# Attention and three graph layers on one core: source scores added by VectorE, own-branch products formed in the layer that uses them

## What is computed

```python
# attention
el, er = scores of every node (8 heads x 4 kinds); em = e_pro @ attn_m
e = (sum_t (el[src] + er[dst] + em) * mask) / 3.0;  e = where(e > 0, e, 0.2 * e)
a = exp(e - max over dst) / sum over dst
rst = segment_sum(feat_src[src] * a, dst)
# each of the three layers
msg = relu(h @ pW + pb)[src]
mean = segment_sum(msg, dst) / max(deg, 1)
out = mean @ lW + lb + h @ rW        # the own branch is h @ rW + lb
h = silu(out / norm(out))            # last layer: layernorm instead of silu
```

## Time and profile before

| | us |
|---|---|
| median of 3 runs | 3454.67 (3454.27 to 3454.99) |
| the profiled execution, its own time | 3451.81 |
| its span, first to last instruction | 3450.0 |
| first gather of the attention (POOL) | 101.68 |
| first gather of the layers | 1457.72 |

### The profile page before, as it was taken

The page is one execution under the profiler, slowest core; times in us unless marked ns, Lnnn a source line. Parts: engine busy times, 40 slices in busy tenths (PEclk is TensorE's granted clock), DMA queues, the critical chain, the costliest instruction groups (busy, mean ns, idle before and its releaser), DMA issues. The chain is left out here.

```text
span 3450.0 us, 44783 instructions
## 1 busy us (share of the span) xinstructions
PE 2900.8 (84%) x12845; PEld 1770.6 (51%) x12845; DVE 1542.9 (45%) x5381; ACT 1377.4 (40%) x3235; POOL 2527.9 (73%) x2655
## 2 busy tenths in 40 slices
PE   7688877777777777199999997999999888999984
PEld 5577656656555655044455553444555433445542
DVE  6399655555555556113333232232333423445445
ACT  5366655555554555033333332333333322222220
POOL 2677777777777777777777776777777767777775
PEclk9688988888888888599999999999999999999995
DMA  7898766666666664166666654666666456667663
GB/s 218 228 281 256 204 171 178 171 169 174 179 168 177 173 169 125 42 195 182 184 194 194 201 173 143 183 180 183 199 196 201 147 171 190 197 199 221 208 187 108
DMA packets 491898, 631.26 MB, mean 183 GB/s; under 512 B 163477, under 2 KB 402096, under 8 KB 491648
## 3 DMA queue, kind: packets, MB, share of 16 engines
q0 software_dynamic: 122192, 324.68, 34.0%
q1 hardware_dynamic: 340848, 277.92, 27.2%
q10 hardware_dynamic: 28608, 25.71, 2.3%
HBM read 558.00 MB, written 70.05 MB: 182 GB/s over the span
## 5 line engine op out<-in xcount | busy, mean ns | idle before, releaser
L1218 POOL DMA_INDIRECT ring<-message_table,src_index x1545 | 1469.8, 951 | 502.5 <-issue 481.1
L1269 PE MATMUL ps<-ring,attention_work 128*128 128x384 f32 (+1 forms) x2940 | 1149.5, 538 | 85.3 <-DMA attention_work<-message_table 75.1
L604 POOL DMA_INDIRECT ring<-attention_table,src_index x784 | 763.1, 973 | 245.6 <-issue 245.2
L1269 PEld LDWEIGHTS ps<-ring,attention_work 128*128 128x128 f32 x2940 | 551.5, 192 | 555.7 <-issue 286.4
L1814 PE MATMUL ps<-ring,one_hot 128*128 128x265 f32 x1568 | 533.1, 458 | 19.7 <-issue 18.6
L1580 ACT ACTIVATE ring<-one_hot 128x384 f32<-128x384 uint8 (+1 forms) x735 | 362.0, 553 | 195.7 <-PE ps L1269 132.9
L1814 PEld LDWEIGHTS ps<-ring,one_hot 128*128 128x128 f32 x1568 | 314.7, 221 | 85.6 <-issue 49.6
L1339 PE MATMUL ps<-ring,attention_work 128*32 128x256 f32 x3090 | 256.6, 402 | 103.7 <-DMA ring<-message_table,src_index 103.4
L613 POOL DMA_INDIRECT dense_adjacency<-times,cell x277 | 269.5, 973 | 84.4 <-issue 84.4
L1434 DVE SCALAR_TENSOR_TENSOR block_o<-ps,inv_deg,root 128x256 f32<-128x256 f32 x147 | 71.1, 484 | 546.8 <-PE ps L1307 546.8
L1783 PE MATMUL ps<-ring,ident 128*128 128x224 f32 x224 | 95.7, 519 | 254.7 <-DMA ring<-attention_table,src_index 254.6
(11 more groups left out here) (185 smaller groups left out, 3500.7 us busy)
## 6 DMA issues: line engine op xcount, KB each, us to landing
attention_work<-message_table SPq DMA_DIRECT2D x360, 256.0 KB
attention_work<-in_dst_edges SPq DMA_DIRECT2D x112, 448.0 KB
ring<-message_table,src_index POOLq DMA_INDIRECT x1545
one_hot<-dense_adjacency SPq DMA_DIRECT2D x63, 336.0 KB, 4.0
one_hot<-dense_adjacency SPq DMA_DIRECT2D x42, 448.0 KB, 4.5
attention_sums<-sums_out SPq DMA_DIRECT2D x112, 132.5 KB
dense_adjacency<-root SPq DMA_DIRECT2D x14, 952.0 KB
ring<-attention_table,src_index POOLq DMA_INDIRECT x784
```

What stands on the lines that cost most here:

```text
L604: pool.indirect_dma_start(m.ring[:, k, t, 0:cols], None, table, bass.IndirectOffsetOnAxis(ap=m.src[:, at:at + 1], axis=0)).then_inc(s[f"ro ...
L1218: pool.indirect_dma_start(m.quad_ring[:, k, j, :], None, m.tables[w.l], bass.IndirectOffsetOnAxis(ap=m.src[:, t:t + 1], axis=0)).then_inc( ...
L1269: last = nc.tensor.matmul(m.ps[:, 2 + half, 0:cols], m.m_rows[:, u % HELD_ROWS, half * P:(half + 1) * P], m.a_rows[:, k, 0:cols], start=(j ...
```

## The change

Three edits.

1. **Source scores.** `left_of` and its identity product are gone from PE. DVE adds the source scores from the gathered rows to the bank and writes the sum to SBUF (`kinds`); the mask multiply then has both inputs in SBUF. Chunk c+3's feature product on PE now waits for that addition of chunk c+2, no longer for the mask multiply.
2. **Own branch.** ACT copies the turned h straight into `root`, which now keeps h transposed. `project` forms 256 columns, the message alone, and DVE adds one bias there. `combine` forms the own branch in the other half of its bank first, ahead of the wait for `merged`; DVE adds its bias in a new instruction after `lmm` and then does the scaled addition. The wait for the zero stores goes from DVE to ACT.
3. **Transposes.** The third transpose of `to_heads` takes 64 edges.

```diff
@@ layers, tensor: combine and project
+            pe.wait_ge(s["o"].sem, s["o"].free(w.slot0 + i))
+            for k in range(2):
+                nc.tensor.matmul(m.ps[:, 0, D:2 * D], m.root[:, n, k * P:(k + 1) * P], m.w_pr[:, w.l, k, D:2 * D],
+                                 start=(k == 0), stop=(k == 1))
             pe.wait_ge(s["merged"].sem, s["merged"].done(w.chunk0 + (q - 1 if q is not None else WORK - 1)))
-            pe.wait_ge(s["o"].sem, s["o"].free(w.slot0 + i))
...
-                last = nc.tensor.matmul(m.ps[:, 5, :], m.b_hT[:, k * P:(k + 1) * P], m.w_pr[:, w.l + 1, k, :],
+                last = nc.tensor.matmul(m.ps[:, 5, 0:D], m.root[:, w.block(i), k * P:(k + 1) * P], m.w_pr[:, w.l + 1, k, 0:D],
@@ layers, vector: first and second
-                nc.vector.tensor_tensor(m.l_msg[:, u % 2, :], m.ps[:, 5, 0:D], m.bias[:, w.l + 1, 0:D], ALU.add)
-                nc.vector.tensor_tensor(m.root[:, n, :], m.ps[:, 5, D:2 * D], m.bias[:, w.l + 1, D:2 * D],
+                nc.vector.tensor_tensor(m.l_msg[:, u % 2, :], m.ps[:, 5, 0:D], m.bias[:, w.l + 1, 0:D],
                                         ALU.add).then_inc(s["evac"].sem, 1)
...
-            nc.vector.scalar_tensor_tensor(m.b_o[:], m.ps[:, 0, 0:D], m.inv_deg[:, n:n + 1], m.root[:, n, :],
+            nc.vector.tensor_tensor(m.b_o[:], m.ps[:, 0, D:2 * D], m.bias[:, w.l, D:2 * D], ALU.add).then_inc(s["rooted"].sem, 1)
+            dve.wait_ge(s["rooted"].sem, s["rooted"].done(u))
+            nc.vector.scalar_tensor_tensor(m.b_o[:], m.ps[:, 0, 0:D], m.inv_deg[:, n:n + 1], m.b_o[:],
@@ attention, tensor
-                pe.wait_ge(s["masked"].sem, s["masked"].done(c - 1))
+                pe.wait_ge(s["added"].sem, s["added"].done(c - 1))
...
-        def left_of(c):
-
-            rows_in(pe, c)
-            nc.tensor.matmul(m.ps[:, 0, 0:TILES * 32].rearrange("p (t n) -> p t n", t=TILES), m.ident[:],
-                             m.ring[:, c % RING, :, WIDE:ROW], start=False, stop=True).then_inc(s["kinds"].sem, 1)
...
-            for j in range(3):
+            for j, edges in enumerate((slice(0, P), slice(0, P), slice(0, P // 2))):
...
-                last = nc.tensor.matmul(m.ps[:, 5, :], m.b_hT[:, k * P:(k + 1) * P], m.w_pr[:, 0, k, :],
+                last = nc.tensor.matmul(m.ps[:, 5, 0:D], m.root[:, n, k * P:(k + 1) * P], m.w_pr[:, 0, k, 0:D],
@@ attention, vector: score_of and biased
+            dve.wait_ge(s["right"].sem, s["right"].done(c))
+            rows_in(dve, c)
+            if c:
+                dve.wait_ge(s["red"].sem, s["red"].done(c - 1))
+            nc.vector.tensor_tensor(m.kinds.rearrange("p (t n) -> p t n", t=TILES),
+                                    m.ps[:, 0, 0:TILES * 32].rearrange("p (t n) -> p t n", t=TILES),
+                                    m.ring[:, c % RING, :, WIDE:ROW], ALU.add).then_inc(s["added"].sem, 1)
             edges_in(dve, c)
-            dve.wait_ge(s["kinds"].sem, s["kinds"].done(c))
-            nc.vector.tensor_tensor(prod4, kinds4, mask4, ALU.mult).then_inc(s["masked"].sem, 1)
+            dve.wait_ge(s["added"].sem, s["added"].done(c))
+            nc.vector.tensor_tensor(prod4, prod4, mask4, ALU.mult).then_inc(s["masked"].sem, 1)
...
-            nc.vector.tensor_tensor(m.root[:, n, :], m.ps[:, 5, D:2 * D], m.bias[:, 0, D:2 * D], ALU.add).then_inc(s["evac"].sem, 1)
@@ attention, scalar: turned
-            nc.scalar.activation(m.b_hT[:], m.ps[:, 4, 0:D], ACT.Copy).then_inc(s["ht"].sem, 1)
+            nc.scalar.activation(m.root[:, n, :], m.ps[:, 4, 0:D], ACT.Copy).then_inc(s["ht"].sem, 1)
```

More of the change, by code:

```diff
@@ L1186 @@
     htrans=1, ht=1, proj=1, evac=1, relu=0, put0=None, put1=None, stats=0, mv=0, square=0, length=0, shift=0, kept0=None,
[L1187 removed]
+    kept1=None, biased=0, scaled=0, out=1, rooted=0, saved0=None, saved1=None)
 def layers(nc, m, a, block, s, stored):
@@ L1794, in to_heads @@
             at, cols = score_at(c), TILES * HEADS
-            for j in range(3):
+            for j, edges in enumerate((slice(0, P), slice(0, P), slice(0, P // 2))):
                 some = at + (j - 1) * HEADS
-                last = nc.tensor.transpose(m.ps[0:cols, 1, j * P:(j + 1) * P], m.score[:, some:some + cols], m.ident[:])
+                last = nc.tensor.transpose(m.ps[0:cols, 1, j * P + edges.start:j * P + edges.stop], m.score[edges, some:some + cols],
+                                           m.ident[edges, edges])
             last.then_inc(s["xt"].sem, 1)
```

21 lines of the change are left out of this document (7 added, 14 removed).

## The result

The changed kernel takes **3461.29 us** (median of 14 runs, 3456.17 to 3462.84) against 3454.10 (14 runs, 3450.05 to 3459.47) for the kernel before, measured side by side: a ratio of 1.0020, 95% interval 1.0013 to 1.0027. That is 7.2 us more, and just at the 0.2% that this measurement can tell from no change. The profiled execution is the fastest of the 14, 3456.17 us with a span of 3454.4, against 3451.81 and 3450.0 before.

A forecast was written before the change was run, and what follows sets the result against it. POOL's back-to-back queue of indirect DMAs was taken as the bound. Stall 1.0 + lock 2.8 - pauses 1.1 and 0.35 + end 1.4 = +3.75 us on the runs' median 3454.67 gave 3458.4 us, range 3453 to 3464.

The forecast's parts named there:

- The bound: Whole kernel: POOL's indirect DMAs run back to back and set the time, so work removed from PE beside them gives nothing.
- The stall in the counting stretch: Attention, 205 to 325 us: DVE's longer steps make POOL wait at its ring, 1.0 us taken, ends 0 and 3.1.
- the credit set against it: Counting stretch: PE saves 0.4 us and on average 0.4 of `project`, DVE enters some 0.5 us earlier, POOL comes later.
- DVE's stretch bites in full: Rival, counting stretch: all counting steps run into each other, 18 x 0.43 = 7.7 us of stall, 3465 us; chance 6%.
- The lock: Attention: the mask multiply, both inputs in SBUF, delays POOL's gather issues; 19% of 112 hit by 0.13 us, 2.8 us.
- in step: Rival, attention: the multiply meets gather issues at a fixed phase, 14.6 us in place of 2.8, 3470 us; chance 11%.
- no lock: Rival, attention: the short multiply never meets the point in POOL's issue, 0 in place of 2.8, 3455.6 us; chance 15%.
- the formula: Attention gathers: lateness is the DVE instruction's end minus the issue's start minus 0.13 us, the point where the issue needs the port.
- The pauses: POOL's restarts after layers 0 and 1: -1.1 us and -0.35 us, giving 15.7 and 15.3 us.
- The end: Last gather to the end: own-branch product +1.0 and DVE's addition +0.45, sum +1.4 us, giving 21.7 us.
- The same additions in the blocks before are off these chains: Pauses: the product and addition added to earlier blocks do not lengthen the chains at the layers' ends; no cost counted.
- Layer 2's room: Layer 2: PE's added 43 us of products fit into its waits; 0 taken. Rival, room too small: 3468 us, 3%.

The follow-up runs named there:

- h1: The changed kernel with the own-branch product issued ahead of the flip and its bias addition ahead of the merge; 4113.4 us on chip C, ratio 0.9934 to before.
- g1: The kernel before, unchanged, run against itself on chip B; 4137.4 us, ratio 0.9981.
- f2: The kernel before with edit 1 alone (source scores added by DVE), on chip B; 4126.7 us, ratio 0.9959 to before.
- g2: The kernel before with edit 1 alone and the counting's long compare (L632) cut into eight; 4116.6 us on chip B, ratio 0.9931 to before.

## Why the prediction was right, and where not

The forecast was 3458.4 us, range 3453 to 3464, "no change" at 80%. The median is 3461.3 us, in the range; the ratio of 1.0020 sits on the border of the 0.2%. By the prediction's steps:

- **The bound** held: POOL's queue back to back, 13.6 us of waits for PE in the whole run, of which some 4.5 us are more than the usual 0.3. That PE's removed work gives nothing held too. Its wait for rows went to DVE's addition, as said:

```profile
L1878 DVE TENSOR_TENSOR attention_work<-ps,ring 128x224 f32<-128x224 f32 x112 | 43.8, 391 | 437.5 <-issue 377.8
```

- **The stall in the counting stretch** was the term that I mis-sized: 1.0 us taken, ends 0 and 3.1, and 4.5 measured, outside the ends. The failed step is "some 11 steps from 205 to 325 us give 11 x 0.28", and the credit set against it. The step is 0.50 us longer and not 0.43, less 0.15 for the bias addition, and the weighting fell back by 0.30 us a step; but DVE had no slack from chunk 8 on, at 190 us, so the delay grew for 12 steps, 3.6 us, up to the weighting of chunk 17, for whose sums the gather of 330.60 waited. The credit for DVE's earlier start was there (1.4 us at chunk 7), but chunk 8's rows took it back and the weighting came out 1.8 us late. So that weighting was 5.5 us late, and the gathers, 1.2 us late by then through longer issues, waited for the rest. What of the 1.8 us is due to the change and what to where L632 met a gather, one pair of profiles can't tell. The rival "DVE's stretch bites in full" (7.7 us, 6%) was nearer than my term, and "wrong if POOL waits for L1820 beyond 5 us" came true: 7.2 by the view, 4.5 beyond the usual.
- **The lock** of 2.8 us: 2.1 us in 17 hits, where 21 were forecast; 1.0 net of what stood at the old multiply. The mechanism held. The sum of the other gathers' excess did not grow (19.5 us before, 19.3 after), since a shift of phase spared some: L1951, as L1949 before, has 5 gathers over 1.02 us with 0.6 us in place of 14 with 2.1. The six hits of L632 went the other way, 13.8 to 14.9 us. So the attention's gathers cost 0.7 us more and not 2.8, and "L604's busy sum grows by 2 to 5 us" was wrong. The rival "in step" (14.6 us) fell, and so did "no lock", though its 0 us are nearer to the 0.7 than my 2.8. By the page "SBUF — State Buffer" of the Trainium skill, section "SBUF: two separate sides", under "Who interferes with whom", a `tensor_tensor` was seen not to stall a DMA; for this DMA, whose offsets lie in SBUF, the 1.16 us at 318.25 say otherwise. One half of the formula needs a correction. The end is sharp: each gather that L632 held, in all the traces, ended 0.82 or 0.83 us behind it. The point of 0.13 us is not, as POOL and DVE after the change show:

```profile
203.63 4.00 POOL L604 DMA_INDIRECT ring<-attention_table,src_index  x1 [0.30 <-issue]
...
203.96 2.85 DVE L632 TENSOR_TENSOR root<-keys 128x2600 f32<-128x2600 f32 x1
```

DVE started 0.33 us behind the issue and held it all the same. Over the traces an L632 that starts from 0.0 to 0.35 us behind an issue sometimes holds it and sometimes doesn't.
- **The pauses** came out at 15.3 us (forecast 15.7) and 16.3 us (forecast 15.3). The gain at the end of layer 0 is the projection at the lower clock, 1.63 us in place of 3.65. At the end of layer 1 the sign was wrong: the copy on ACT came 1.1 us later behind the last gather (the rows above), held up by the block before. The rest, -0.5 us, is near the forecast of -0.35.
- **The end** was +2.0 and not +1.4, with the parts wrong both ways. From gather to end: own product between flip and combine +0.95 (forecast 1.0), addition +0.46 (0.45), a combine 0.15 shorter. Not foreseen: ACT's copy waiting 1.77 us where it waited 0.06, +1.7. Given back, in this execution: the last rows landed 2.81 us behind the start of their gather in place of 3.37, and the sum ran at 2.4 GHz, 0.63 us in place of 1.07, together -1.0. The step that failed, here and at the end of layer 1, is "The same additions in the blocks before are off these chains": the last two blocks are in series by way of ACT's list. At the end of layer 0 it did not bite: there ACT's copy was not late (PE's flip waited the same 0.49 us for it).
- **Layer 2's room** held: 0 taken, 1.2 us measured in its gathers, with 1.2 us gained in layer 1's.

So 3.75 us forecast and 6.3 measured: the stall +3.5 and the end and the pauses +1.1 above my terms, the attention's gathers 2.1 below. The total was in the range partly by that, which is luck.

## What to carry to other kernels

Where one engine is 96% busy and feeds the ring of the bounding queue, count an added instruction in every step of the filled stretch at its pitch, beginning where the engine last stood idle, and give no credit for a head start that the next wait for data takes back. An instruction added to a block's chain costs at the end once for each block that is still in series there: look in the in-order queues of the engines that seem idle (here ACT's) for what stands ahead of the last copy. And work whose inputs are ready early belongs ahead of the wait and not behind it; h1 took back what edit 2 had cost in pauses and end. And before a variant is read on another chip, look whether the same engine is the bound there.

## What the runs showed of the hardware

The same kernel takes 3454 us in the runs of the result and 4138 to 4146 us on chips A, B and C, with indirect DMAs of the same length on POOL (L604 0.973 us, 0.967 in g1) and moving the same 631 MB, at 183 and 153 GB/s over the span. The gathers' packets end 2.7 and 3.0 us behind the issue, so it is not the rows that are late there. PE stands idle for 496 us in place of 17 where the profile shows nothing that it waits for; what holds it is open. It turns the change's signs: the changed kernel's attention is 5 us longer in the result, and 18 us shorter on chips A to C with edit 1.

A DVE instruction with both inputs in SBUF holds an indirect DMA that POOL is issuing: the DMA ends 0.82 to 0.83 us behind the end of an instruction of 2.85 us (L632), in every hold of the traces. With L632 cut in eight, one gather of over 1.8 us is left where f2 has five (g2).

And one kernel against itself, 12 runs against 28, came out at 0.9981 with an interval that barely reaches 0.9999. Read by themselves, such intervals claim more than they hold.
